# A software-pipelined decoder layer: PSUM banks chosen per job and tile before and after the steady turns, new orders there, first loads on two queues

## The reference

```python
qkv = x @ W_attn                              # 16 heads of 8
att = q @ k / sqrt(8), causal
att = polymax(att)                            # x > 0: x^2 + 1; -100 <= x <= 0: 1 - x/100; all / 1000
x = layernorm(x + (att @ v) @ W_proj)
q, k, v = x @ WQ, ctx @ WK, ctx @ WV          # 16 heads of 64
x = layernorm(x + softmax(q @ k / 8) @ v @ WO + bO)
probs = softmax(x @ router_w.T + router_b)    # 16 experts, the best 6 are kept and renormalized
x = layernorm(x + sum_e gate[e] * (x @ expert_w[e]))
```

## Time and profile before

| | us |
|---|---|
| median of 3 runs | 1014.57 |
| lowest, highest | 1012.44, 1014.77 |
| the profiled execution | 1011.26 |
| its span, first to last instruction | 1009.5 |
| head: until PE starts the first steady turn | 143.9 |
| 25 steady turns on PE | 734.8 |
| tail: from PE's first job of `LAST` to the end | 130.8 |

### The profile page before, as it was taken

The page is one execution under the profiler, slowest core; times in us unless marked ns, Lnnn a source line. Parts: engine busy times, 40 slices in busy tenths (PEclk is TensorE's granted clock), DMA queues, the critical chain, the costliest instruction groups (busy, mean ns, idle before and its releaser), DMA issues.

```text
span 1009.5 us, 47204 instructions
## 1 busy us (share of the span) xinstructions
...
## 2 busy tenths in 40 slices
...
DMA packets 41882, 21.19 MB, mean 21 GB/s; under 512 B 18912, under 2 KB 40928, under 8 KB 41824
## 3 DMA queue, kind: packets, MB, share of 16 engines
...
## 4 chain that ended last, share of the span: by engine, by line
PE 66%; DVE 17%; issue 11%; ACT 3%; DVEq 1%; POOL 1%; DMA 0%; ACTq 0%; SPq 0%; POOLq 0%
PE ps L447 61%; DVE sums L888 4%; PE ps L572 4%; DVE allowed L852 3%; DVE p L864 2%; DVE stats L805 1%; DVE residual L888 1%; ACT prob L764 1%; DVE mv L811 1%; DVE best L911 1%; PE ps L595 1%; DVE ps L859 1%; DVEq L354 0%; ACT qm L636 0%; DVE left L920 0%
## 5 line engine op out<-in xcount | busy, mean ns | idle before, releaser
L888 DVE SCALAR_TENSOR_TENSOR sums<-ps,gate,sums 128x128 f32<-128x128 f32 x896 | 239.9, 340 | 18.5 <-PE ps L447 17.7
L996 POOL TENSOR_TENSOR p<-p,rowinv 128x1024 f32<-128x1024 f32 x64 | 121.8, 1904 | 219.1 <-DVE rowinv L841 219.0
L447 PE MATMUL ps<-wo_sb,oT 128*128 128x128 f32 x1024 | 127.5, 278 | 0.6 <-issue 0.6
L447 PEld LDWEIGHTS ps<-wo_sb,oT 128*128 128x128 f32 x1024 | 121.1, 192 | 5.4 <-issue 1.0
L636 ACT ACTIVATE v<-ps 128x512 f32<-128x512 f32 x128 | 76.3, 598 | 50.2 <-PE ps L447 45.2
L447 PE MATMUL ps<-ex_hi,x2T_hi 128*128 128x512 f32 x256 | 110.4, 431 | 3.3 <-POOL x2T_lo L978 3.1
L636 ACT ACTIVATE oT<-ps 128x512 f32<-128x512 f32 x128 | 69.6, 597 | 45.7 <-PE ps L447 45.1
L756 ACT ACTIVATE x<-residual,shift,rstd 128x128 f32<-128x128 f32 x192 | 83.7, 484 | 26.9 <-POOL shift L991 17.5
L447 PE MATMUL ps<-ex_lo,x2T_hi 128*128 128x512 f32 x256 | 101.7, 397 | 0.0
L447 PE MATMUL ps<-ex_hi,x2T_lo 128*128 128x512 f32 x256 | 101.5, 396 | 0.0
L852 DVE SCALAR_TENSOR_TENSOR allowed<-ps,const 128x512 f32<-128x512 f32 x128 | 87.1, 681 | 15.2 <-ACT relu L659 13.6
...
## 6 DMA issues: line engine op xcount, KB each, us to landing
...
```

Source lines behind the costliest of these rows:

```text
L447: return pe.matmul(o, l, r, start=start, stop=stop)
L888: done = V.scalar_tensor_tensor(after, ps(f"FF{4 * r + q}")[:, C * e:C * e + C], gate[:, r, 4 * q + e:4 * q + e + 1], before, ALU.mult, AL ...
L996: G.tensor_tensor(weights, weights, rowinv[:, r].unsqueeze(2).broadcast_to([P, H, T]), ALU.mult).then_inc(p2_ready, 1)
```

## The change

Head and tail get new orders on PE, ACT, DVE and POOL (SP's only in the head). On each engine the steps of the head are the same 152, 165, 151 and 49, those of the tail the same 145, 112, 167 and 85; the lists of the steady turns keep their text. A second table gives some jobs of given tiles another bank than `JOBS` has. Two loads move from SP's queue to ACT's, and the k weights are loaded ahead of v and q. PE does four products of zeros before its first wait. A way to let ACT and POOL share the experts' sums of the last tiles is there, but with `SHARED = 0` no step uses it, and `wait_summed` waits for what was waited for before.

```diff
+SHARED = 0
+WARM = 4
-("heads0", "P0", None), ("heads1", "P1", None), ("heads2", "P2", None),
+("heads0", "P0", None), ("heads1", "P0", None), ("heads2", "P0", None),
+OTHER_BANK_FIRST = """
+    Q@0=B3 Q@2=B3 Q@4=B1 Q@6=B4 K@0=B6 K@1=B5 K@3=B1 K@4=B6 K@5=B5 K@6=B4 V@0=B1 V@1=B2 V@2=B2 V@4=B0 V@5=B1 V@6=B2 S1_0@0=B0
+    S1_0@1=B5 S1_0@2=B6 S1_0@4=B1 S1_0@5=B4 S1_1@0=B5 S1_1@1=B6 S1_1@2=B7 S1_1@3=B5 S1_1@4=B4 S1_1@5=B5 S1_2@0=B3 S1_2@1=B0
...
 FIRST = {
     "SP": """
-        x_columns@1 context@1 x_rows@1 x_columns@2 x_columns@3 x_columns@4 x_rows@2 context@2 x_columns@5 x_rows@3 x_columns@6
+        x_columns@1 x_columns@2 x_columns@3 context@1 x_rows@1 x_rows@2 x_columns@4 x_columns@5 context@2 x_rows@3 context@3
...
     "PE": """
-        Q@0 K@0 S1_0@0 S1_1@0 S1_2@0 S1_3@0 V@0 heads1@0 heads2@0 heads0@0 K@1 Y@0 Q@1 V@1 PR@0 S1_0@1 S1_1@1 S1_2@1 S1_3@1 V@2 K@2
-        K2_2@0 K2_3@0 K2_1@0 Q@2 K2_0@0 Y@1 S1_0@2 S1_1@2 S1_2@2 S1_3@2 PR@1 X1T@0 Q2_0@0 K@3 Q2_2@0 Q2_3@0 Q2_1@0 V@3 S2_0@0 Q@3
-        V2_2@0 S2_1@0 Y@2 S1_0@3 V2_3@0 V2_1@0 S1_1@3 V2_0@0 S1_2@3 S1_3@3 X1T@1 K2_2@1 PR@2 K2_0@1 K2_1@1 K@4 Q2_0@1 PT0a@0 K2_3@1
-        Q2_1@1 Q2_3@1 PT1b@0 Q2_2@1 PT1a@0 PT0b@0 Q@4 S2_0@1 AC0@0 S2_1@1 Y@3 V@4 AC1@0 V2_3@1 V2_1@1 V2_2@1 V2_0@1 S1_0@4 S1_1@4
+        V@0 K@0 Q@0 heads1@0 S1_0@0 S1_1@0 S1_2@0 S1_3@0 heads2@0 heads0@0 Q@1 V@1 K@1 S1_0@1 Y@0 S1_1@1 S1_2@1 S1_3@1 Q@2 PR@0 V@2
+        K@2 K2_2@0 K2_0@0 S1_0@2 S1_1@2 Q@3 S1_2@2 S1_3@2 K@3 X1T@0 Y@1 K2_1@0 S1_0@3 Q2_2@0 K2_3@0 Q2_3@0 S1_1@3 S1_2@3 S1_3@3
+        Q2_1@0 Q2_0@0 PR@1 V2_1@0 S2_0@0 V2_0@0 V@3 V2_3@0 S2_1@0 V2_2@0 K@4 Q@4 Y@2 V@4 K2_2@1 K2_0@1 X1T@1 K2_1@1 K2_3@1 Q2_1@1
+        S1_0@4 Q2_0@1 S1_1@4 PR@2 S1_2@4 S1_3@4 K@5 Y@3 Q2_2@1 PT0b@0 PT0a@0 Q2_3@1 AC0@0 Q@5 S2_0@1 V2_0@1 PT1a@0 PT1b@0 V2_2@1
...
     "ACT": """
-        queries@0 kK@0 relu0@0 square0@0 relu1@0 square1@0 relu2@0 square2@0 relu3@0 square3@0 experts_hi@0 mV@0 heads_hi1@0
-        heads_hi2@0 kK@1 heads_hi0@0 mY@0 queries@1 mV@1 relu0@1 square0@1 relu1@1 square1@1 relu2@1 norm1@0 square2@1 relu3@1
+        mV@0 kK@0 queries@0 heads_hi1@0 relu0@0 square0@0 relu1@0 square1@0 relu2@0 heads_hi2@0 square2@0 relu3@0 square3@0 queries@1
+        heads_hi0@0 kK@1 experts_hi@0 mV@1 mY@0 relu0@1 square0@1 relu1@1 queries@2 relu2@1 square1@1 square2@1 kK@2 relu3@1
+        square3@1 mK2_2@0 mK2_0@0 norm1@0 relu0@2 queries@3 x1_hi@0 kK@3 relu1@2 square0@2 square1@2 mY@1 mV@2 relu2@2 mK2_1@0
...
 LAST = {
     "PE": """
-        WO0@-3 FF6@-5 V2_2@-2 FF2@-5 X2T@-4 WO1@-3 V2_0@-2 V2_3@-2 PT0b@-2 LG@-4 PT0a@-2 FF3@-5 K2_2@-1 K2_3@-1 X1T@-1 K2_0@-1
-        K2_1@-1 Q2_2@-1 Q2_0@-1 PT1b@-2 PT1a@-2 Q2_1@-1 FF0@-4 AC0@-2 FF4@-4 Q2_3@-1 V2_1@-1 AC1@-2 S2_0@-1 X2T@-3 FF5@-4 FF1@-4
+        WO0@-3 K2_2@-1 K2_0@-1 WO1@-3 FF0@-5 FF4@-5 K2_3@-1 PT0a@-2 X2T@-4 X1T@-1 FF1@-5 FF5@-5 Q2_0@-1 Q2_3@-1 FF2@-5 FF6@-5 Q2_1@-1
+        Q2_2@-1 PT1b@-2 PT0b@-2 S2_0@-1 AC0@-2 S2_1@-1 V2_3@-1 PT1a@-2 LG@-4 FF7@-5 FF3@-5 V2_1@-1 AC1@-2 WO0@-2 FF0@-4 FF4@-4 FF5@-4
...
-def banks_of(job):
+def banks_of(job, tile):
+    bank = OTHER_BANK.get((job, tile), BANK[job]) if isinstance(tile, int) else BANK[job]
...
             load_columns(0)
-            sp.dma_start(w_attn_sb[:], w_attn).then_inc(attn_in, 16)
-            sp.dma_start(const[:], consts).then_inc(const_in, 16)
-            for dst, src, arrived in zip(heads_ld, (wq_t, wk_t, wv_t), heads_in):
-                sp.dma_start(dst, src).then_inc(arrived, 16)
+            sp.dma_start(heads_ld[1], wk_t).then_inc(heads_in[1], 16)
             load(cT, ctx_t, cT_in, 0)
+            sp.dma_start(heads_ld[2], wv_t).then_inc(heads_in[2], 16)
+            sp.dma_start(heads_ld[0], wq_t).then_inc(heads_in[0], 16)
...
+            pe.wait_ge(zeroed, 1)
+            rows_of_zeros = vp[:].rearrange("p b g n -> p (b g n)")
+            for _ in range(WARM):
+                mm(pairs[0][:, 0:P], rows_of_zeros[:, 0:P], rows_of_zeros[:, 0:P])
             pe.wait_ge(attn_split, 1)
...
+            nc.scalar.dma_start(w_attn_sb[:], w_attn).then_inc(attn_in, 16)
+            nc.scalar.dma_start(const[:], consts).then_inc(const_in, 16)
             act.wait_ge(attn_in, 16)
```

More of the change, by code:

```diff
@@ new lines @@
+        Q2_1@0 Q2_0@0 PR@1 V2_1@0 S2_0@0 V2_0@0 V@3 V2_3@0 S2_1@0 V2_2@0 K@4 Q@4 Y@2 V@4 K2_2@1 K2_0@1 X1T@1 K2_1@1 K2_3@1 Q2_1@1
+        S1_0@4 Q2_0@1 S1_1@4 PR@2 S1_2@4 S1_3@4 K@5 Y@3 Q2_2@1 PT0b@0 PT0a@0 Q2_3@1 AC0@0 Q@5 S2_0@1 V2_0@1 PT1a@0 PT1b@0 V2_2@1
+        AC1@0 S2_1@1 V2_3@1 V2_1@1 WO0@0 WO1@0 K2_1@2 K2_0@2 K2_2@2 PR@3 X1T@2 K2_3@2 V2_0@2 Q2_2@2 Q2_0@2 PT0a@1 PT0b@1 Q2_1@2
+        Q2_3@2 AC0@1 S2_0@2 PT1b@1 PT1a@1 S2_1@2 V2_1@2 V2_3@2 V2_2@2 V@5 Y@4 K2_3@3 K2_1@3 S1_0@5 AC1@1 S1_1@5 WO0@1 S1_2@5 S1_3@5
@@ L100 @@
[L100 to L107, removed]
@@ new lines @@
+        mQ2_2@0 square2@2 relu3@2 mQ2_3@0 square3@2 relu0@3 mK2_3@0 mQ2_1@0 mQ2_0@0 relu1@3 square0@3 mV2_1@0 mV2_0@0 square1@3
+        exp0@0 mV2_3@0 relu2@3 square2@3 mV2_2@0 norm1@1 kK@4 queries@4 mV@3 relu3@3 square3@3 mY@2 x1_hi@1 mK2_0@1 mK2_2@1 mK2_1@1
+        mK2_3@1 exp1@0 mQ2_0@1 mQ2_1@1 relu0@4 relu1@4 kK@5 square0@4 mV@4 mQ2_2@1 mPT0b@0 mPT0a@0 square1@4 mQ2_3@1 mY@3 mAC0@0
+        queries@5 mV2_0@1 mPT1a@0 mPT1b@0 relu2@4 relu3@4 square2@4 mAC1@0 mV2_3@1 exp0@1 square3@4 mV2_2@1 exp1@1 mV2_1@1 mK2_1@2
@@ new lines @@
+        norm1@2 x1_hi@2 mK2_0@2 mK2_3@2 norm2@0 mK2_2@2 mQ2_2@2 mQ2_0@2 mPT0b@1 mPT0a@1 mQ2_1@2 mQ2_3@2 mV2_0@2 mAC0@1 mPT1b@1
+        mPT1a@1 mV2_1@2 exp0@2 exp1@2 mV@5 mK2_3@3 mK2_1@3 mV2_3@2 mAC1@1 mV2_2@2 mY@4 relu0@5 square0@5 relu1@5 mK2_2@3 relu2@5
+        square1@5 mPT0b@2 square2@5 norm1@3 mPT0a@2 mX2T@0 x1_hi@3 relu3@5 mK2_0@3 mAC0@2 mQ2_0@3 mQ2_1@3 square3@5 mQ2_2@3 mQ2_3@3
+        logit_exp@0 mV2_1@3 queries@6 mPT1a@2 mPT1b@2 exp0@3 mV2_2@3 base3@0 mAC1@2 norm2@1 exp1@3 mV@6 kK@6 mY@5 mX2T@1
@@ L115 @@
[L115 to L122, removed]
+        heads_lo1@0 allow0@0 pieces0@0 allow1@0 p1_0@0 pieces1@0 allow2@0 p1_1@0 heads_lo2@0 allow3@0 pieces2@0 pieces3@0 p1_2@0
@@ L136 @@
     "PE": """
[L137 to L140, removed]
@@ L145 @@
[L145 removed]
+        V2_0@-4 PT0b@-4 S1_0@-1 LG@-6 X1T@-3 PR@-2 S1_1@-1 V2_3@-4 S1_2@-1 S1_3@-1 PT0a@-4 K2_3@-3 Q2_1@-3 Q2_0@-3 K2_2@-3 Q2_2@-3
+        K2_1@-3 PT1a@-4 PT1b@-4 K2_0@-3 Q2_3@-3 AC0@-4 V2_2@-3 V2_1@-3 V2_0@-3 AC1@-4 S2_0@-3 S2_1@-3 V2_3@-3 WO0@-4 WO1@-4 X2T@-5
+        K2_3@-2 K2_0@-2 K2_1@-2 K2_2@-2 LG@-5 X1T@-2 FF4@-6 FF0@-6 Q2_0@-2 Q2_1@-2 Q2_2@-2 Q2_3@-2 Y@-1 S2_0@-2 PT0b@-3 PT0a@-3
+        FF5@-6 FF6@-6 FF1@-6 AC0@-3 FF2@-6 V2_0@-2 V2_1@-2 V2_3@-2 V2_2@-2 S2_1@-2 PT1a@-3 PR@-1 PT1b@-3 K2_1@-1 FF7@-6 FF3@-6 AC1@-3
```

278 lines of the change are left out of this document (172 added, 106 removed), and 2 rows, old and new, of the table JOBS.

## The result

| | median | runs | ratio to before, 95% interval |
|---|---|---|---|
| before | 1014.67 us | 1012.44 to 1016.0 | |
| changed | 1003.25 us | 1001.8 to 1004.65 | 0.9889 [0.9866, 0.9913] |

What follows compares the result with a forecast made beforehand. Turns bound by PE's work; head by waits among engines, then PE from about 60 us. Head 4.7 plus tail 1.3 gave 6.0 us less, forecast 1008.6 against 1014.57; its own range 1005 to 1011.5, overall 1002 to 1016.

Steps and rivals of the forecast that it cites:

- The loads: Start of the head: x of tile 1 lands 0.4 us earlier, at 20.0, within bounds of 20.4 and 19.3.
- 0.4 or less: Loads: by the skill's rule on queues, the landing of x of tile 1 moves by 0.4 us or less.
- Around half a us each: Loads: cost of an issue on SP's queue; with two fewer, x_columns@1 is issued about 1 us earlier.
- The head up to S2_0@1: Head, walked step by step: relu0@1 at 28.2, S2_0@0 at 48.7, S2_0@1 at 71.0, 4.7 us ahead counting extra work.
- `experts_hi` has moved into the way: Head, on ACT: experts_hi, earlier in an idle place, now precedes relu0@1, so that wins only 0.9 us.
- x of tile 2 and of the banks: Head: x of tile 2 comes earlier; bank releases set S1@2 at 35.5 and the first Q2 at 41.7.
- The head behind S2_0@1: Rest of the head: 3.7 us less work, waits and clock losses as before; ends at 139.2, 4.7 us less.
- The turns: The 25 steady turns of 734.8 us: change 0, within 1.5 us.
- The tail: End of the kernel: work unchanged, part of 7.5 us idle time goes; 1.3 us less, between 6 less and 2 more.
- The idle time of the tail goes too: Rival on the tail: head gives 4.7 us and tail 7.5, for 1002.4 us; chance 0.15.
- ACT did not become the bound: Slower rival: ACT bounds the head, AC1@0 comes at 85.3, 3.3 us past 82.0, for 1017.9 us; chance 0.15.
- Does not do what it says: Rival on the head: earlier weights start nothing earlier, only relu0@1's 0.9 us stays, for 1013.7 us; chance 0.20.

Runs made afterwards that it cites:

- e3: The changed kernel with all loads on SP's queue again in their old order; ratio 0.9896 to the kernel before.
- e5: The changed kernel with x of tile 1 issued on SP right after x_sb, ahead of the experts and eight small loads; 996.75 us, ratio 0.9825 to before.
- e4: The changed kernel with experts_hi@0 put back ahead of queries@1 on ACT; ratio 0.9902 to the kernel before.
- e2: The changed tail with head, loads and head banks of the kernel before, no products of zeros; ratio 0.9966 to the kernel before.
- e1: The changed head and loads with the tail's lists and banks of the kernel before; ratio 0.9933 to the kernel before.
- e6: The changed kernel with DVE's tail list putting tile 31's attended, stats2 and var2 behind two weighs again; ratio 0.997 to the kernel before.
- e8: The changed kernel with e6's DVE list, other banks for some tail jobs, and X2T and LG of tile 31 later on PE; ratio 0.9924 to before.

## Why the prediction was right in its sign and short in its size

The time, 1003.25, lies below the range that the prediction gave its own sum (1005 to 1011.5) and inside the wider one (1002 to 1016).

**The loads.** x of tile 1 was forecast for 20.0, with 19.3 as the lower bound; it came at 18.96. The bound stood on the earlier trace rows, where POOL's split began 4.3 us after the issue; here it began 3.4 after it. The prediction cited a rule of the Trainium skill, DMA: Bandwidth & Descriptors, section Issuing engines are not separate DMA queues, by which a second queue saves issue time alone. The runs agree with it: with two queues the issue came 1.25 us sooner in the mean and the split 1.4 sooner (six profiles against three, as above), and e3 lost nothing that its interval can tell. But "0.4 or less" does not follow from the rule, which leaves the whole of the issue time to be won. "Around half a us each" does not hold for all of SP's issues: that of `w_proj` took 5.42 us, and 5.20 in the kernel before. What no part of the prediction saw is that the place in one queue was worth more than the second queue: e5 took 5.2 us off the head by it.

**The head up to S2_0@1.** `relu0@1` was forecast for 28.2 and came at 28.20, for another reason than I gave: the match is luck. "`experts_hi` has moved into the way" is wrong: e4 took it out and won nothing. ACT waited for S1@1, which ended at 28.18. x of tile 1 had come late (PE stood idle for 5.00 us ahead of Q@1), and PE took 1.67 us for S1@1, against 1.20 in the earlier trace rows, at a granted clock of 0.57:

```profile
24.60:28.20 3.60, 3.55 (x129) 3.21 (x129) 0.68 (x1) 2.94 (x5) 2.98 (x3) 0.57 0.04 8
```

From there the walk through ACT's, DVE's and the banks' releases was right within about 1 us down to AC1@0. That fits what the prediction said of x of tile 2 and of the banks; no run took either of them out.

**The head behind S2_0@1.** This is the term that was mis-sized: "I let it lose as much to waits and clock as the old one did: 71.0 + 71.9 - 3.7 = 139.2". The head ended at 133.76. Of the 5.4 us between 139.2 and that, 0.8 is the earlier S2_0@1. The rest, 63.52 instead of 71.91 - 3.7 = 68.2, splits by PE's rows: busy time fell by 66.81 - 60.70 = 6.1 instead of 3.7, and idle time by 5.10 - 2.82 = 2.3 instead of 0. Against e2's execution of the old head, at full clock, busy time fell by 4.7: so the work done ahead was 1.0 more than I had counted, 1.4 was the slower clock of the one execution of before that I walked from, and 2.3 is idle time that I had carried over. In time the head is worth 6.8 (e1) and not 4.7.

**The turns.** Forecast 0 within 1.5; the profiles gave 2.6 more. In eleven profiles of kernels with the same turns, the first two took 61.6 to 64.5 us and turns 3 to 24 took 643.5 to 646.4; the change lies inside both spreads (63.1 and 645.0, before 61.6 and 643.9).

**The tail.** "1.3 us less, between 6 less and 2 more" holds the 3.4 that e2 measured. The mechanism fits the rows: two weighs now cover the last tile's chain, and DVE's idle time behind `weigh0` of tile 29 fell from 4.54 to 2.00 us. How much of the gain is this, and not the banks or ACT's order, e6 and e8 leave open. Its size was wrong: the prediction let only the short stops ahead of `weigh0@-1` and its like go, but the old order took 3.2 to 5.6 us more than the new one behind `weigh0` of tile 29 in its three profiles.

**The rivals.** "The idle time of the tail goes too" forecast 1002.4, 0.8 from the time, by way of a head of 4.7 and a tail of 7.5; they were 6.8 and 3.4 (e2) to 4.5 (the whole change less e1), so its time is near and its split is not. ACT did not become the bound: AC1@0 came at 74.49, well before 82.0. "Does not do what it says" fell with e1 and e2.
